# Norm and quantisation of the last network's inputs, moved into attention 1 for sequences 0 to 5

## The reference

```python
h = _layernorm(x) * (1 + ca) + sa
x = x + ga * attention(h)
h = _layernorm(x) * (1 + cb) + sb
x = x + gb * network(h)
```

```python
scale = max(max(abs(xb)) / 6, 1e-12)
q = GRID[searchsorted(MID, abs(xb / scale))] * sign(xb) * scale
gate, y = fp4_linear(x, w_gate), fp4_linear(x, w_up)
return fp4_linear(silu(gate) * y, w_down)
```

## Time and profile before

| | us |
|---|---|
| median of 3 runs (lowest, highest) | 1404.31 (1404.12, 1406.02) |
| the profiled execution, its own time | 1409.18 |
| its span | 1407.4 |
| PE busy in the span | 1040.1 (74%) |
| DVE busy | 811.7 (58%) |
| ACT busy | 612.5 (44%) |
| POOL busy | 469.5 (33%) |
| attention 1, about | 1000 to 1221 |
| network 1, about | 1222 to 1407 |

### The profile page before, as it was taken

The page is one execution under the profiler, slowest core; times in us unless marked ns, Lnnn a source line. Parts: engine busy times, 40 slices in busy tenths (PEclk is TensorE's granted clock), DMA queues, the critical chain, the costliest instruction groups (busy, mean ns, idle before and its releaser), DMA issues. The chain is left out here.

```text
span 1407.4 us, 25467 instructions
## 1 busy us (share of the span) xinstructions
PE 1040.1 (74%) x8506; PEld 695.0 (49%) x8506; DVE 811.7 (58%) x1755; ACT 612.5 (44%) x2039; POOL 469.5 (33%) x319
## 2 busy tenths in 40 slices
PE   2589988898989898976322786764399999546765
PEld 1245656565656565656212453533166666425544
DVE  4266666666666666555558132122346564488986
ACT  1257675767676767661002222211155555223232
POOL 1424242424232323211003688876100000134551
PEclk9589999999999999985556897887599999767778
DMA  8334343434343434322101243363200000000000
GB/s 255 83 91 115 97 112 81 120 83 121 82 122 81 122 81 122 83 70 84 40 21 47 57 70 62 57 143 27 63 1 1 1 0 1 1 0 8 16 15 23
DMA packets 85373, 93.56 MB, mean 66 GB/s; under 512 B 18752, under 2 KB 58032, under 8 KB 85312
## 3 DMA queue, kind: packets, MB, share of 16 engines
q1 hardware_dynamic: 73184, 81.50, 22.1%
q0 software_dynamic: 11840, 10.76, 5.2%
q10 hardware_dynamic: 288, 0.53, 0.1%
HBM read 24.36 MB, written 10.70 MB: 25 GB/s over the span
## 5 line engine op out<-in xcount | busy, mean ns | idle before, releaser
L736 POOL TENSOR_TENSOR qk_cos<-qk_raw,const 128x512 f32<-128x512 f32 x128 | 182.1, 1423 | 361.2 <-ACT qk_raw L560 361.2
L549 ACT ACTIVATE prob<-psS,neg_max 128x96 f32<-128x96 f32 x512 | 167.5, 342 | 65.4 <-DVE neg_max L621 65.3
L459 PE MATMUL psQ<-a_xnT,weights 128*128 128x512 f32 x256 | 152.6, 679 | 21.9 <-ACT v_tok L565 18.4
L524 PEld LDWEIGHTS psO<-probT,v_windows 96*64 96x64 f32 x2048 | 71.5, 140 | 117.8 <-ACT probT L598 94.0
L1320 POOL DMA_INDIRECT sums<-ex_y,ex_index x64 | 102.8, 1606 | 37.3 <-issue 18.3
L636 DVE TENSOR_TENSOR qk_roped<-qk_cos,qk_swapped 128x512 f32<-128x512 f32 x128 | 107.3, 838 | 5.1 <-DVE qk_swapped L627 4.6
L1310 POOL DMA_INDIRECT ex_rows<-rows,ex_index x64 | 66.6, 1040 | 127.4 <-DMA ex_index<-lists 108.2
L549 ACT ACTIVATION_READ_ACCUMULATOR prob<-psS,neg_max 128x1 f32 x512 | 106.0, 207 | 0.0
L560 ACT COPY qk_raw<-psQ 128x512 f32<-128x512 f32 x128 | 75.5, 590 | 69.7 <-PE psQ L459 69.7
L524 PE MATMUL psO<-probT,v_windows 96*64 96x64 f32 x2048 | 89.3, 231 | 21.9 <-ACT probT L598 21.4
L598 ACT COPY probT<-psT 96x512 f32<-96x512 f32 x128 | 74.8, 585 | 55.0 <-PE psT L504 55.0
(11 more groups left out here) (282 smaller groups left out, 2065.2 us busy)
## 6 DMA issues: line engine op xcount, KB each, us to landing
qk_swapped<-qk_raw SPq DMA_DIRECT2D x512, 64.0 KB, 2.0
v_windows<-v_tok SPq DMA_DIRECT2D x32, 384.0 KB, 4.4
v_windows<-v_tok SPq DMA_DIRECT2D x32, 256.0 KB, 3.6
mod<-mod_rows SPq DMA_DIRECT2D x8, 512.0 KB, 7.5
ex_w<-in_L_ffn_W SPq DMA_DIRECT2D x16, 256.0 KB
v_windows<-v_tok SPq DMA_DIRECT2D x32, 96.0 KB, 2.1
x<-in_L_attn_x POOLq DMA_DIRECT2D x4, 512.0 KB, 12.6
rows<-rt_h SPq DMA_DIRECT2D x8, 256.0 KB, 2.4
```

The source lines that it names most:

```text
L459: last = nc.tensor.matmul(psQ[:, :], k.wqkvT[:, col:col + P], xnT[:, :], start=True, stop=True)
L524: ins = nc.tensor.matmul(psO[D * j:D * j + D, u % 2, i * P + a * HALF:i * P + (a + 1) * HALF], vw[:, par, a, t, hd], probT[:, 2 * j + i, a ...
L549: last = nc.scalar.activation(prob[:, s, 2 * j + i, :], psS[:, s, j, i * KW:(i + 1) * KW], ACT.Exp, bias=nmax[:, s, 2 * j + i:2 * j + i + ...
L736: nc.gpsimd.tensor_tensor(rcos[:, half, :], raw[:, half, :], k.const[:, K_COS:K_COS + T], ALU.mult).then_inc(cos_done, 1)
```

## The change

For sequences 0 to 5 (`EARLY` = 6) the norm, the modulation and the quantisation of network 1's input run inside attention 1. In body `b` VectorE finishes the statistics of sequence `b - 1` in unit 5 (two units after its residual) and normalises it in unit 7 into a new buffer `a1_h2`; GpSimd takes the root and modulates it; and in body `b + 1`, so for sequence `b - 2` of the running body, VectorE does the ten quantisation steps: one behind each unit's multiply, two in units 1 and 6. Step 1 waits for GpSimd's second modulation. The quantised inputs are written to `k.total`, whose old content is no longer needed; network 1 transposes from there.

In network 1 only inputs 6 and 7 are still normalised, modulated and quantised, in bodies 4 and 5, beside the hidden quantisation as before. Bodies 0 to 3 quantise the hidden result alone, each step then waiting for the one before it. GpSimd takes the root for the last 8 columns in one operation. The loops of both phases are gone: all eight bodies are written out on every engine.

```diff
+def fp4_steps(nc, dve, own, q):
+    v = nc.vector
+    dve.wait_ge(*q.ready)
+    done = own.mark(v.tensor_reduce(q.amax, q.source_blocks, AX.X, ALU.max, apply_absolute_value=True))
+    yield
+    dve.wait_ge(own.sem, done)
+    done = own.mark(v.tensor_scalar(q.scale, q.amax, 1.0 / 6.0, 1e-12, ALU.mult, ALU.max))
+    yield
...
+    dve.wait_ge(own.sem, done)
+    own.mark(v.tensor_tensor(q.out_blocks, q.total_blocks, q.scale_wide, ALU.mult))

 phase_attention1, all engines
-        def turns(eng, body):
-            for b in range(2):
-                body(b, b, b == 0, True, True)
-            with eng.Fori(1, B // 2 - 1) as pair:
-                for i in range(2):
-                    body(pair * 2 + i, i, False, True, True)
-            for b in range(B - 2, B):
-                body(b, b % 2, False, b < B - 1, False)
+        def turns(body):
+            for b in range(B):
+                body(b, b % 2, b == 0, b < B - 1, b < B - 2)

 phase_attention1, GpSimd
             def body(b, par, first, next1, next2):
                 if next2:
                     norm.root_one(pool, b + 2)
+                if 0 <= b - 1 < EARLY:
+                    norm2.root_one(pool, b - 1)
+                    modulate2(b - 1)

 phase_attention1, VectorE
             def body(b, par, first, next1, next2):
+                steps = quantise2(b - 2) if 0 <= b - 2 < EARLY else iter(())
                 for u in range(U1):
...
                     if u == 4 and next2:
                         modulate(b + 2)
+                    if u == 5 and 0 <= b - 1 < EARLY:
+                        finish2(b - 1)
+                    next(steps, None)
+                    if u in (1, 6):
+                        next(steps, None)
+                    if u == 7 and 0 <= b - 1 < EARLY:
+                        normalise2(b - 1)

 phase_ffn1, TensorE
-                    last = nc.tensor.transpose(psX[:, t * P:(t + 1) * P], xq[:, t, :], k.ident)
+                    last = nc.tensor.transpose(psX[:, t * P:(t + 1) * P], k.total[:, b, t, :], k.ident)

 phase_ffn1, GpSimd
-            norm.root(pool, 0)
-            modulate(0)
-            norm.root(pool, 1)
-            modulate(1)
+            norm.root_late(pool)
             product(0, 0)
             def body(b, par, first, last, ahead):
-                if ahead:
+                if EARLY <= b + 2 < B:
                     modulate(b + 2)

 phase_ffn1, VectorE
-            for b in range(2):
-                normalise(b)
-                x_job.ready = (modulated, 2 * b + 2)
-                wait(dve, x_turned, b)
-                last, = fp4(nc, dve, own, [x_job])
-                last.then_inc(xq_ready, 1)
             def body(b, par, first, last, ahead):
-                if ahead:
+                job = x_jobs.get(b + 2)
+                if job:
                     normalise(b + 2)
```

More of the change, by code:

```diff
@@ L1054, in fp4 @@
     return last
+def fp4_steps(nc, dve, own, q):
[7 more added lines that the diff above has]
+    dve.wait_ge(own.sem, done)
+    done = own.mark(v.reciprocal(q.inv, q.scale))
+    yield
+    dve.wait_ge(own.sem, done)
+    done = own.mark(v.tensor_scalar(q.inv, q.inv, BELOW, None, ALU.mult))
+    yield
+    dve.wait_ge(own.sem, done)
+    done = own.mark(v.tensor_tensor(q.xn_blocks, q.source_blocks, q.inv_wide, ALU.mult))
+    yield
+    dve.wait_ge(own.sem, done)
+    done = own.mark(v.tensor_scalar(q.binade.bitcast(U32), q.xn.bitcast(U32), EXPONENT, None, ALU.bitwise_and))
+    yield
+    dve.wait_ge(own.sem, done)
+    done = own.mark(v.tensor_scalar(q.binade, q.binade, 1.0, None, ALU.max))
+    yield
+    dve.wait_ge(own.sem, done)
+    done = own.mark(v.scalar_tensor_tensor(out=q.total, in0=q.binade, scalar=MAGIC, in1=q.xn, op0=ALU.mult, op1=ALU.add))
+    yield
+    dve.wait_ge(own.sem, done)
+    done = own.mark(v.scalar_tensor_tensor(out=q.total, in0=q.binade, scalar=-MAGIC, in1=q.total, op0=ALU.mult, op1=ALU.add))
+    yield
+    dve.wait_ge(own.sem, done)
+    own.mark(v.tensor_tensor(q.out_blocks, q.total_blocks, q.scale_wide, ALU.mult))
 FP4_SIGNALS = 9
@@ L1531, in body @@
                     out_project(b, par)
-            turns(pe, body)
+            turns(body)
         @block.scalar
@@ L1580, in body @@
                     copy_oT(b, par, TILES - 1)
-            turns(act, body)
+            turns(body)
         @block.sync
@@ L1591, in _, with modulate2 @@
         def _(pool):
+            def modulate2(b):
+                wide = lambda j: k.mod[:, j, b, :].unsqueeze(1).to_broadcast([P, TILES, C])
+                pool.wait_ge(normed2, b + 1)
+                nc.gpsimd.tensor_tensor(h2[:, :, :], h2[:, :, :], wide(CB), ALU.mult).then_inc(modulated2, 1)
+                pool.wait_ge(modulated2, 2 * b + 1)
+                nc.gpsimd.tensor_tensor(h2[:, :, :], h2[:, :, :], wide(SB), ALU.add).then_inc(modulated2, 1)
             norm.root_one(pool, 0)
@@ L1597, in body @@
                     norm.root_one(pool, b + 2)
-            turns(pool, body)
+                if 0 <= b - 1 < EARLY:
+                    norm2.root_one(pool, b - 1)
+                    modulate2(b - 1)
+            turns(body)
         @block.vector
@@ L1629, in residual, with finish2, normalise2, quantise2 @@
                 measure(nc, k, own, b)
+            def finish2(b):
+                dve.wait_ge(own.sem, own.base + own.n)
+                norm2.finish_one(dve, own, b)
+            def normalise2(b):
+                norm2.normalise(dve, own, b, h2[:, :, :]).then_inc(normed2, 1)
+            def quantise2(b):
+                flat = lambda t: t.rearrange("p t c -> p (t c)")
+                job = Fp4(flat(h2[:, :, :]), flat(k.total[:, b, :, :]), TILES * C, x_bufs)
+                job.ready = (modulated2, 2 * b + 2)
+                return fp4_steps(nc, dve, own, job)
             own.turn(0)
@@ L1665, in body @@
                         modulate(b + 2)
+                    if u == 5 and 0 <= b - 1 < EARLY:
[5 more added lines that the diff above has]
+                        normalise2(b - 1)
                 if not next1:
                     residual(b)
-            def first_two():
-                own.turn(0, OWN_FIRST)
-                for b in range(2):
[L1672 to L1683, removed]
+            turns(body)
 def phase_ffn1(nc, k):
@@ L1702, in phase_ffn1, with turns @@
         normed, modulated, gated_up = sem("normed"), sem("modulated"), sem("product")
-        per = (TILES - 1) + 2 * FP4_SIGNALS
-        own = Tally(sem("own"), 2 * per)
-        OWN_FIRST = 6 + 2 * (TILES - 1 + FP4_SIGNALS)
+        own = Tally(sem("own"))
         block = ctx.enter_context(nc.Block())
[L1708 to L1723, removed]
+        def turns(body):
+            for b in range(B):
+                body(b, b % 2, b == 0, b == B - 1, b < B - 2)
         @block.tensor
@@ L1854, in body @@
                     store(b)
-            turns(sp, body)
+            turns(body)
             sp.wait_ge(k.stored, 16 * B)
@@ L1860, in _ @@
         def _(dve):
-            x_job = Fp4(h[:, :, :].rearrange("p t c -> p (t c)"), xq[:, :, :].rearrange("p t c -> p (t c)"), TILES * C, x_bufs)
+            flat = lambda t: t.rearrange("p t c -> p (t c)")
+            x_jobs = {b: Fp4(flat(h[:, :, :]), flat(k.total[:, b, :, :]), TILES * C, x_bufs) for b in range(EARLY, B)}
             h_jobs = [Fp4(silu[:, par, :, :].rearrange("p t f -> p (t f)"), hq[:, :, :].rearrange("p t f -> p (t f)"),
@@ L1865, in normalise @@
             def normalise(b):
-                wait(dve, xq_ready, b)
+                wait(dve, xq_ready, b - EARLY)
                 norm.normalise(dve, own, b, h[:, :, :]).then_inc(normed, 1)
@@ L1889, in body @@
                 wait(dve, h_turned, b * TILES)
[L1890 to L1893, removed]
+                if job:
+                    job.ready = (modulated, 2 * (b + 2 - EARLY) + 2)
+                    h_last, x_last = fp4(nc, dve, own, [h_jobs[par], job])
                     h_last.then_inc(hq_ready, 1)
@@ L1902, in body @@
                     residual(b)
-            turns(dve, body, own)
+            turns(body)
 def phase_store(nc, k):
```

23 lines of the change are left out of this document (14 added, 9 removed).

## The result

| | before | after |
|---|---|---|
| median of 3 runs (lowest, highest), us | 1404.31 (1404.12, 1406.02) | 1384.71 (1382.39, 1388.94) |
| the profiled execution / its span | 1409.18 / 1407.4 | 1382.39 / 1380.6 |
| first transposes of attention 1 at | 1004.99 | 993.70 |
| attention 1, from there to network 1's first statistics | 217.0 | 221.0 |
| network 1, from there to the end | 185.4 | 165.9 |

The ratio is 0.9861 (95% interval 0.9822 to 0.9901): faster by 19.6 us, where 28.6 were forecast, and 1.7 us outside the range. In two later sets of runs the same kernel had 0.9816 (0.9783 to 0.9849) and 0.9832 (0.9778 to 0.9887). So the sign was right and the size too large.

A forecast was written before the change was run, and what follows sets the result against it. TensorE was taken to bound attention 1 and VectorE network 1; 29.1 us saved less 0.5 in attention gave 28.6, so 1380.6 for the profiled execution and 1375.7 for the median, range 1368.5 to 1383.

The forecast's parts named there:

- attention 1, cost of the added work: Attention 1: stalls of 0.0 to 0.1 us per sequence where TensorE's unit 6 waits for VectorE's multiply, 0.5 us in all.
- end of h 0: Network 1: the first hidden quantisation starts at 1234.6, takes 11.25 us plus 3.0 standing for GpSimd's product, ends at 1248.9.
- three periods, h 0 to h 3: Network 1, from first to fourth hidden quantisation: two periods of 14.6 and one of 17.0 meeting GpSimd's product, 46.2 us.
- bodies 4 and 5, together: Network 1, bodies still carrying inputs 6 and 7: 20.6 us each as before, the first 0.3 less, ending at 1336.0.
- from h 5's end on: Network 1 after the sixth hidden quantisation, whose end moves from 1365.1 to 1336.0: nothing changes from there.
- The added wait: Attention 1: step 1 waits for GpSimd's modulations, starts about 2 us into unit 1's time, and is covered.
- rival D: Attention 1: stalls cost TensorE its clock, a sequence's 24.6 us become 49; with two of them 1425 us; chance 3%.
- rival A: Network 1: GpSimd takes the port in each of the three periods, 50.7 to 53 instead of 46.2, 1380 to 1382; 20%.
- this knife edge: Network 1: GpSimd's product starts just behind the quantisation at low clock, but at 11.7 to 12.5 us, inside its last sums, at full.

The follow-up runs named there:

- after_again: The changed kernel run again with nothing altered, for a second trace: ratio 0.9816 to the kernel before, network 1 165.4 us.
- after_b: The changed kernel run a third time with nothing altered: ratio 0.9832 to the kernel before, network 1 158.1 us.
- halves: The changed kernel with each hidden quantisation run as two halves of 704 elements in turn, so steps overlap: ratio 0.9753 to the kernel before.
- lumped: The changed kernel with all ten quantisation steps of a sequence behind unit 6 of attention 1: ratio 1.0078 to the kernel before, attention 1 247.1 us.
- halves_b: The kernel of halves run a second time: ratio 0.9780 to the kernel before, attention 1 227.1 us, network 1 153.9 us.
- halves_gapped: The kernel of halves with each half's step again waiting for the step just before it: ratio 1.0003 to the kernel before, network 1 184.7 us.

## Why the prediction was wrong in size and right in kind

Point by point, times from the start of network 1's block, predicted and measured in the first trace:

| step | predicted | measured | off by |
|---|---|---|---|
| attention 1, cost of the added work | 0.5 | 0.04 | -0.5 |
| end of h 0 | 26.9 | 27.7 | +0.8 |
| three periods, h 0 to h 3 | 46.2 | 50.2 | +4.0 |
| bodies 4 and 5, together | 40.9 | 40.8 | -0.1 |
| each of them | 20.3, 20.6 | 17.5, 23.3 | -2.8, +2.7 |
| from h 5's end on | 42.3, "nothing changes" | 47.2 | +4.9 |
| network 1 | 156.3 | 165.9 | +9.6 |

**Attention** was right. The added wait showed as 1.0 us of VectorE's time in each of six sequences, and nothing of it reached TensorE; one row of VectorE's timeline of the changed kernel (L1068 is the first added step, L1639 the second modulation):

```profile
1119.78 0.69 DVE L1068 TENSOR_REDUCE a1x_amax<-a_h 128x32 f32<-128x512 f32 x1 [0.97 <-POOL a_h L1639]
```

One size was off without harm: 7.3 us per sequence were counted from the spacing of steps that wait for each other; dealt between other operations they overlap with these, and VectorE's busy time grew by 30.1 / 6 = 5.0 per sequence, to 75% and not 90%. The run with all steps in one place shows that TensorE's slack, and not VectorE's idle 40%, is what the change lives on, and it bears out rival D's price of a lost clock, though not in the changed kernel.

**h 0** stood 2.8 us in its mask step, 3.0 predicted.

**Three periods**: from result to result 17.4, 14.6 and 18.2 us; two of three met a product, where I took one. This step failed: the term of 46.2 measured 50.2 here and 50.1 in after_again. It measured 47.4 in after_b, with one of three met, exactly the case that I had taken; so the number of meetings, and not only its forecast, varies between executions. The mechanism is that of rival A, in two periods of its three; it was described and given 20%, because the 7.97 us of the earlier trace rows seemed to speak against it. They did not. That product met a quantisation of two jobs in turn, whose steps overlap, and the change itself takes the second job away and so opens the gaps. Over all traces, 20 products began in a quantisation where the next step came behind a gap of some 0.03 us, and every one was let in ahead of that step. I had both halves of this in the text and still weighed them as evidence on one question. The Trainium skill's rule ("SBUF — State Buffer", section "Who interferes with whom"), that whoever issues first gets the port pair and the other fully blocks, was right for steps with gaps: the products that began at 1231.41, 1254.76 and 1347.29 were let in at the running step's end. It does not by itself say what halves shows, that a product can stay out over several step ends when the steps overlap.

**Bodies 4 and 5** came out right by luck. Body 4 was 2.8 us short, since its product had already met h 3 (1286.29) and the normalisation did not stand (2.07 us); body 5 was 2.7 long, since a mask step stood beside the product at 1323.77 on top of the normalisation (4.34).

**"From there on nothing changes"** is the step that failed outright in the first trace. h 6 has no input beside it either, before and after. Before, its product came 0.1 us after the quantisation (1381.31), behind a down projection at low clock (5.1 us); after, the down projection ran at full clock, the product came 0.5 us before the last step (1347.29) and that step stood, 2.8 us. The last down projection then met low clock, 5.19 us instead of 2.92, and closes the stage. First the kernel before, below the dots the changed kernel:

```profile
1370.48 5.13 PE L1756 MATMUL f_psY<-wdT,f_hqT 128*128 128x128 f32 x24 [0.71 <-ACT f_hqT L1801]
1379.58 1.63 DVE L1053 TENSOR_TENSOR f_hq<-f1h_total,f1h_scale 128x1408 f32<-128x1408 f32 x1
1399.68 2.92 PE L1756 MATMUL f_psY<-wdT,f_hqT 128*128 128x128 f32 x24 [0.71 <-ACT f_hqT L1801]
...
1338.68 2.92 PE L1801 MATMUL f_psY<-wdT,f_hqT 128*128 128x128 f32 x24 [0.71 <-ACT f_hqT L1846]
```

The code was unchanged, but its timing against the clock was not. The prediction had named exactly this knife edge for h 1 to h 3 and did not apply it to h 6. In after_again the same part took 47.2 us too; in after_b it took 42.3, to the tenth what was predicted, with the product behind h 6 and the last down projection at 2.92. So the step was wrong as a certainty: it holds in one of the three traces of the changed kernel.

**The clock** also decides attention 1's length before any of the change matters. Over all traces but that of lumped it is about 215.3, 217.0, 221.0 or 227.0 us with the same steady stretch; TensorE's clock rose for good 20.6 us (halves) to 45.3 us (halves_b) after the stage's first transposes. In the first trace after it cost 4.0 us against the one before. A range of 14.5 us around one forecast left too little room for this, and the profiled executions differ by 11.3 us already at the start of attention 1, in stages that the change does not touch; what causes that is open. By luck these nearly cancel in one number: the profiled execution was forecast at 1380.6 and took 1382.39, with 11.3 us less ahead of attention 1, 3.5 more in it than forecast and 9.6 more in network 1.

## What to carry to other kernels

Work moved under a saturated TensorE was free here as long as each piece was smaller than the slack to the next instruction that TensorE waits for; past it, 7.7 us of stalls made the stage 27 us longer, through the clock. Before taking one of two interleaved jobs away from VectorE, ask what their overlap held off: single steps with waits between them let GpSimd's products in, each time. A transfer of work that changes only the arrival time of a GpSimd operation still changes who waits, so either order it by a semaphore or price every quantisation, not only those the diff edits. Here one execution's trace could not price it: three traces of one kernel gave 165.9, 165.4 and 158.1 us.

## What the runs showed of the hardware that I had not expected

A VectorE gap of 0.03 to 0.04 us between steps with SBUF inputs was enough for a waiting GpSimd operation of 3.2 us to get in, in 20 of 20 cases. Where the steps overlap by 0.08 us, the outcome went mostly by the step in which the product began. Outside halves_gapped, none of 24 products that began in a sum or a last product, with a step still to come, was let in before the quantisation had ended; they took 4.59 to 8.63 us. Of 14 that began in a maximum, a first product or a mask step, 13 were let in at the running step's end or the one after it, as at 1323.77 above. The fourteenth began 0.44 us before the next mask step, as that one did, and took 10.31 us (lumped, 1366.18). In halves_gapped three products that began in a last sum or a last product were let in across an overlap. So the gap is not the whole rule, and by which rule a product is let in across an overlap is open.

One idle of TensorE of 1.32 us, after 70 us without any, was followed by 10 us at 1.2 GHz, and an equal one 31 us later was not.
